# Inverse blocks of the first and last batch turned on VectorE, prologue in another order, joins over four partition groups

## Chip, cores and metric

The kernel runs on one core of a Trainium2 chip. The metric is the device time of one execution in microseconds, taken as the median of several runs. The core has five engines that work from their own queues in order: TensorE (PE, with its weight loads as PEld), VectorE (DVE), ScalarE (ACT), GpSimd (POOL) and SyncE (SP), which here issues all DMAs. They meet only in semaphores.

## What is computed

The input x is 8 batches of 512 tokens with 128 channels in float32. Half a gated feed-forward network (FFN), a gated delta-rule attention block with its own MLP, and half the same FFN again are added to it:

```python
x = x + 0.5 * ffn(layernorm(x))
x = x + attn(layernorm(x))
x = x + 0.5 * ffn(layernorm(x))

# attn: q, k are silu projections of unit length (8 heads of 128), v a silu projection
def step(S, inp):
    q_t, k_t, v_t, a_t, b_t = inp
    kS = jnp.einsum('bhk,bhkv->bhv', k_t, S)
    bk = (b_t[..., None] * k_t)[..., :, None]
    S = a_t[..., None, None] * (S - bk * kS[..., None, :]) + bk * v_t[..., None, :]
    o = jnp.einsum('bhk,bhkv->bhv', q_t, S)
    return (S, o)
```

The FFN is a silu-gated layer from 128 to 512, two gelu layers of 512x512 and one back to 128. All of it stays in float32.

## The kernel before

The recurrence over 512 tokens is cut into NC = 4 chunks of C = 128 tokens. With H = 8 heads that makes U = 32 units per batch, and for each unit a triangular 128x128 system has to be inverted. The inverse ends in R (as left operand of `solve`, line 1537).

**The inverse.** `decayed_k0` and `decayed_k` write the system into R. SyncE's `blocks` sends the four 32x32 diagonal blocks of each unit to `blocks_out`, `blocks_in` brings them back as blkA, now with block and unit (4 x 32) on the 128 partitions. GpSimd's `invert` runs 31 steps of two instructions (lines 580 and 583) on blkT, and then writes the transposed inverse over blkA (line 586). SyncE's `back` sends blkT to t_back and blkA to r_back, waits, and reads them as 32x32 blocks: T into TB by three DMAs, the other into the diagonal of R by four. Four joins on TensorE then build the off-diagonal parts: `join` 0 and 1 work on 32x32 tiles (lines 1873 and 1875), joins 2 and 3 on 64x64 tiles (lines 1881 and 1883). The results of a join lie in banks 6 and 7 (x = 0 and 1, 16 units each), and `joined` on VectorE and ScalarE copies them into TB and R, for the next join and for `solve`. In joins 0 and 1 one bank is filled after the other, and its results alternate between two of the four groups of 32 output partitions.

**The stages.** The order is written out by hand on every engine; nothing is planned by a scheduler. Batch 0 has a prologue, `P_alone`, that exists on every engine: it mixes the first FFN of batch 1 (`f1_slots`, 20 slots), the turns of keys (`turn0(1, c)`) and queries (`turn0(0, c)`), the key products `keys_keys0`, the projections `proj0` and the query products `keys_queries0`. Then come the norm of batch 1 (`N_T`, `N_logits`, `N_sums`), ten projections of batch 1 done ahead (AHEAD) and the four `lone_join`, each with one product of one column ahead of it (`hold`, line 1851). The loop over t = 1 to 5 has the recurrence SP of batch t-1 with the projections of batch t, the first FFN of batch t+1 (`F1`) and the second FFN of batch t-1 (`F2`), between whose slots the joins of batch t stand (JOIN_SLOTS). The last batch's inverse runs beside the second FFN of batch 6, with its joins at LATE_SLOTS 11, 13, 16 and 18, and `SP_tail` follows.

**What waits for what.** In the prologue the first join waits for the three TB DMAs (b_TB), join 1 for the four R DMAs (b_Rin). `SP_first`, the first `solve`, waits for the copies of join 3. `keys_keys` of batch 1 reads KT, which is made by `squares` (VectorE), a power (GpSimd, line 537), `unit_k` (VectorE, lines 811 and 817) and then a store and a load through k_rows. `turn0(0, 0)` waits for `unit_q0(0)`, eight scalings on ScalarE (line 1267) after the reciprocal root of `norms0(0)` on VectorE. TB also holds the gated output of batch 1's first FFN until slot 7 has read it, so VectorE clears a part of it only then (line 898).

## Time and profile before

| | us |
|---|---|
| median of 3 runs (1413.53 to 1416.9) | 1413.98 |
| profiled execution, whole | 1415.69 |
| profiled execution, span | 1414.0 |
| TensorE busy | 1381.2 |
| VectorE busy | 836.1 |
| ScalarE busy | 665.3 |
| GpSimd busy | 570.0 |

The span is the profile's time from the first to the last instruction. A busy time over several stages says little about a single wait: the view of the waits names who ended an idle stretch, the chain shows the steps one after the other, the timeline gives start and length of groups of instructions with the idle time ahead of them, and the view by stretches has the granted clock of TensorE as a share of 2.4 GHz. A float32 matmul appears as two records, so `x128` at line 1873 are 64 matmuls. In the timeline a group's time reaches to the modelled end of its last matmul and overlaps the next group a little; the chain's pieces add up.

### The profile page before, as it was taken

To read this page: it belongs to the slowest core of one execution; us is meant where nothing else is said; L and a number is where in the kernel's file an instruction comes from. 1 tells how busy PE (TensorE), PEld (TensorE's weight loads), DVE (VectorE), ACT (ScalarE), POOL (GpSimd) and SP (SyncE) were. 2 spreads that over 40 slices of the span, in tenths; PEclk is the share of its full clock that TensorE was granted. 3 is DMA by queue.
4 is the path that set the end of the run, shared out by engine and by line. 5 is a ranking of instruction groups with operands and counts; after the bars stand their busy time and mean duration, and the time that the engine had idled before them with its cause. 6 is when DMAs were issued, how large, how long until landed. Compare 5 with 4: busy or idle time off the path is not lost.

```text
span 1414.0 us, 25147 instructions
## 1 busy us (share of the span) xinstructions
PE 1381.2 (98%) x9760; PEld 957.4 (68%) x9760; DVE 836.1 (59%) x2480; ACT 665.3 (47%) x1138; POOL 570.0 (40%) x646
## 2 busy tenths in 40 slices
PE   9999999999999999999999999999999999999998
PEld 5456676657866588566875668656786657864987
DVE  3566677455864566743776548756486445771452
ACT  2567556226652366424573256622566236642233
POOL 0028252831448134561346504284143822566100
PEclk9999999999999999999999999999999999999999
DMA  5120355532554235640447304473155332643000
GB/s 183 55 66 16 89 127 121 95 87 64 133 104 104 52 84 128 119 108 17 119 110 138 86 24 109 103 133 87 41 127 117 79 84 68 146 110 78 17 1 8
DMA packets 359607, 125.00 MB, mean 88 GB/s; under 512 B 325312, under 2 KB 340416, under 8 KB 359488
## 3 DMA queue, kind: packets, MB, share of 16 engines
q1 hardware_dynamic: 359488, 123.40, 37.9%
q8 instruction: 77, 1.26, 0.4%
q14 instruction: 42, 0.34, 0.1%
HBM read 79.58 MB, written 43.78 MB: 87 GB/s over the span
## 4 chain that ended last, share of the span: by engine, by line
PE 77%; POOL 9%; issue 6%; DVE 4%; DMA 2%; ACT 1%; SPq 1%; POOLq 0%; DVEq 0%; ACTq 0%
PE bank L1367 25%; PE bank L1478 9%; PE bank L1396 4%; PE bank L1564 4%; PE bank L1573 4%; PE bank L1537 4%; POOL blkT L583 4%; POOL blkP L580 3%; PE bank L1503 3%; PE bank L1375 3%; PE bank L1554 3%; PE bank L1545 3%; PE bank L1528 3%; PE bank L1520 3%; PE bank L1777 1%
## 5 line engine op out<-in xcount | busy, mean ns | idle before, releaser
L1367 PE MATMUL bank<-big,h 128*128 128x512 f32 (+1 forms) x1056 | 445.9, 571 | 2.3 <-DMA TB<-t_back 2.3
L1367 PEld LDWEIGHTS bank<-big,h 128*128 128x128 f32 x1056 | 195.2, 191 | 194.9 <-issue 186.1
L537 POOL TENSOR_TENSOR rnorm<-ssq,mhalf 128x16 f32<-128x16 f32 (+1 forms) x35 | 84.1, 2403 | 454.4 <-DVE ssq L806 454.4
L1478 PE MATMUL bank<-wqkv,nT 128*128 128x512 f32 x336 | 162.4, 604 | 1.1 <-ACT V L1193 1.1
L583 POOL TENSOR_TENSOR blkT<-blkT,blkP 128x31 f32<-128x31 f32 (+15 forms) x248 | 134.4, 542 | 19.4
L580 POOL TENSOR_TENSOR blkP<-blkA,blkT 128x31 f32<-128x31 f32 (+15 forms) x248 | 129.2, 521 | 32.0 <-DMA blkA<-blocks_out 13.2
L1396 PE MATMUL bank<-xT,w 128*128 128x512 f32 (+1 forms) x272 | 117.2, 573 | 9.2 <-DVE big L707 6.3
L1106 ACT ACTIVATE big<-bank,cols 128x512 f32<-128x512 f32 (+1 forms) x68 | 43.9, 662 | 136.1 <-PE bank L1367 98.2
L1114 ACT ACTIVATE big<-bank,cols 128x512 f32<-128x512 f32 (+1 forms) x68 | 44.0, 661 | 130.0 <-PE bank L1367 130.0
L913 DVE TENSOR_TENSOR MT<-bank,MT 128x512 f32<-128x512 f32 x56 | 38.5, 691 | 100.4 <-PE bank L1520 100.4
L564 POOL TENSOR_TENSOR QET<-QET,sgf 128x1024 f32<-128x1024 f32 x24 | 56.5, 2352 | 102.4 <-DMA sgf<-e_rows 102.4
L1396 PEld LDWEIGHTS bank<-xT,w 128*128 128x128 f32 x272 | 48.7, 190 | 61.1 <-issue 41.5
L1478 PEld LDWEIGHTS bank<-wqkv,nT 128*128 128x128 f32 x336 | 57.8, 194 | 42.6 <-issue 37.6
L546 POOL TENSOR_TENSOR MT<-rows_or_g,maskf 128x1024 f32<-128x1024 f32 x28 | 77.2, 2755 | 13.7 <-PE bank L1564 13.4
L1183 ACT ACTIVATE MT<-MT,biasj 128x128 f32<-128x128 f32 x256 | 78.2, 389 | 0.5 <-POOL MT L546 0.2
L1537 PEld LDWEIGHTS bank<-V,R 128*128 128x128 f32 x512 | 61.5, 192 | 11.7 <-issue 9.8
L1193 ACT ACTIVATE big<-bank 128x512 f32<-128x512 f32 x56 | 32.5, 597 | 77.2 <-PE bank L1478 77.1
L1375 PEld LDWEIGHTS bank<-w,big 128*128 128x128 f32 x512 | 62.5, 192 | 8.6 <-issue 7.9
L1564 PEld LDWEIGHTS bank<-MT,V 128*128 128x128 f32 x512 | 61.3, 192 | 9.6 <-issue 9.6
L1573 PEld LDWEIGHTS bank<-wo,blkA 128*128 128x128 f32 x512 | 61.2, 192 | 8.7 <-issue 8.6
L1375 PE MATMUL bank<-w,big 128*128 128x128 f32 x512 | 66.9, 278 | 0.0
L1520 PEld LDWEIGHTS bank<-QET,KT 128*128 128x128 f32 x448 | 56.4, 192 | 13.4 <-issue 13.4
(221 smaller groups left out, 2458.5 us busy)
## 6 DMA issues: line engine op xcount, KB each, us to landing
rows_or_g<-g_rows SPq DMA_DIRECT2D x28, 512.0 KB, 5.0
q_rows<-mid SPq DMA_DIRECT2D x28, 512.0 KB, 4.9
QET<-q_rows SPq DMA_DIRECT2D x112, 128.0 KB, 4.3
k_rows<-R SPq DMA_DIRECT2D x27, 512.0 KB, 2.8
KT<-k_rows SPq DMA_DIRECT2D x108, 128.0 KB, 3.7
sgf<-e_rows SPq DMA_DIRECT2D x24, 512.0 KB, 4.8
blocks_out<-R SPq DMA_DIRECT2D x128, 32.0 KB, 1.7
blkA<-blocks_out SPq DMA_DIRECT2D x8, 512.0 KB, 3.8
```

The costliest lines, as they stand in the source:

```text
L537: pool.tensor_tensor(rnorm[:, heads_of], ssq[:, heads_of], mhalf[:, :].to_broadcast([128, heads_of.stop - heads_of.start]), ALU.pow).then_ ...
L580: pool.tensor_tensor(prod, A3[:, j, j + 1:].unsqueeze(2).to_broadcast([128, n, m]), T3[:, j:j + 1, 0:m].to_broadcast([128, n, m]), ALU.mul ...
L583: pool.tensor_tensor(T3[:, j + 1:, 0:m], T3[:, j + 1:, 0:m], prod, ALU.subtract).then_inc(b_prod, 1)
L1183: last = act.activation(MT[:, u, :], MT[:, u, :], ACT.Exp, bias=biasj[:, u:u + 1])
L1367: last = pe.matmul(bank[bk + i][:, t], w[:, k, 128 * o:128 * o + 128], src[:, k, t], start=(k == 0), stop=(k == KB - 1))
L1375: last = pe.matmul(bank[4][:, 128 * c:128 * c + 128], src[:, k, 128 * c:128 * c + 128], w[:, k, :], start=(k == 0 and c == chunks[0]), sto ...
L1396: pe.matmul(bank[bk][:, t], w[:, 128 * o:128 * o + 128], xT[:, t], start=True, stop=True).then_inc(f["gate"], 1)
L1478: pe.matmul(bank[proj_bank(b, n)][:, :], nT[:, 128 * c:128 * c + 128], wqkv[:, i // 2, 512 * (i % 2):512 * (i % 2) + 512], start=True, sto ...
L1520: last = pe.matmul(heads(bank[query_bank(b, c, g)])[:, h, :], KT[:, u, :], QET[:, u, :], start=True, stop=True)
L1537: last = pe.matmul(heads(bank[g])[:, h, :], R[:, u, :], V[:, u, :], start=True, stop=True)
L1564: last = pe.matmul(heads(bank[2 + g])[:, h, :], V[:, u, :], MT[:, u, :], start=(c == 0 and h == 0), stop=True, skip_group_check=True)
L1573: last = pe.matmul(bank[2][:, 0:D], oT[:, hh, :], wo[:, hh, :], start=(hh == 0), stop=(hh == H - 1))
```

## The change

Batches 0 and 7 (`turned(b)`) no longer go through t_back and r_back. GpSimd's `invert` ends without the transposed copy, `back` is not called for them on SyncE, and VectorE reads blkT itself by 32x32 block transposes: `turn_T` (one instruction of 128x1024 for the left half of TB), `turn_T1` (32x1024) and four `turn_R` (32x1024 each, one for each diagonal block of R). The joins of these batches wait for b_turn. Joins 0 and 1 of all batches (`join_quarters`) now alternate between banks 6 and 7, and the output groups go round all four: the two banks use different halves. Both banks of such a join are complete at its end only, so `joined` waits for both at k < 2, and reads the group that `at` names. `unit_q0(0)` becomes one VectorE instruction. The rest is order: the third and fourth key turn and the last key products of the prologue come before slots 6 and 7, the first query turn comes after the last slot; join 0 stands before the ahead projections; the norm of xin for batch 2 goes from the joins to the stretch of `decayed_k0`; the squares of batch 1 go before the last copies.

```diff
+def turned(b):
+    return b in (0, B - 1)
...
                 sp.wait_ge(b_prod, b * 2 * (BS - 1) + 2 * (BS - 1))
                 sp.dma_start(t_back.rearrange("p u i c -> (p u) (i c)"), blkT[:, :]).then_inc(b_Tout, 16)
-                sp.wait_ge(b_R, b + 1)
+                sp.wait_ge(b_R, b)
...
-            e_store(0), load_xin(2), load_x1(1), P_alone(), e_load(0, 1), back(0), scaled_rows(0), rows(1), grow_in(1, 0)
+            e_store(0), load_xin(2), load_x1(1), P_alone(), e_load(0, 1), scaled_rows(0), rows(1), grow_in(1, 0)
...
-            P(B - 1), back(B - 1), scaled_rows(B - 1), store(B - 2)
+            P(B - 1), scaled_rows(B - 1), store(B - 2)
...
+                if turned(b):
+                    return
                 pool.wait_ge(b_prod, b * steps + steps)
...
+            def turn_T(b):
+                dve.wait_ge(b_prod, (b + 1) * 2 * (BS - 1))
+                dve.transpose(TB[:, :, 0:BS].rearrange("i u c -> i c u"), T_ci).then_inc(b_turn, 1)
+
+            def turn_T1(b):
+                r = slice(BS, 2 * BS)
+                dve.transpose(TB[r, :, r].rearrange("i u c -> i c u"), T_ci[r]).then_inc(b_turn, 1)
+
+            def turn_R(b, p):
+                r = slice(BS * p, BS * p + BS)
+                dve.transpose(R[r, :, r].rearrange("c u i -> c i u"), T_ic[r]).then_inc(b_turn, 1)
...
+            def joins_alone():
+                turn_T(0), turn_R(0, 1), gates_abs(1), turn_R(0, 3), joined(0, 0)
+                turn_T1(0), joined(0, 1), gates_log(1)
+                turn_R(0, 2), joined(0, 2), turn_R(0, 0), cumulated(1), squares(1, 0), joined(0, 3)
+                N_rows(1, n0, 0, n_n0)
...
-            for k in range(JOINS):
-                joined(B - 1, k)
+            turn_T(B - 1), turn_R(B - 1, 1), turn_R(B - 1, 3), joined(B - 1, 0), turn_T1(B - 1), joined(B - 1, 1)
+            turn_R(B - 1, 2), joined(B - 1, 2), turn_R(B - 1, 0), joined(B - 1, 3)
...
-                turn0(1, 1), keys_keys0(0)
+                turn0(1, 1), keys_keys0(0), turn0(1, 2)
                 f1_slots(5)
-                turn0(1, 2), keys_keys0(1)
-                f1_slots(6)
-                turn0(1, 3), keys_keys0(2)
-                f1_slots(7)
-                keys_keys0(3), proj0(0, 0)
+                keys_keys0(1), turn0(1, 3), keys_keys0(2), keys_keys0(3)
+                f1_slots(6, 7)
+                proj0(0, 0)
...
+            def join_quarters(k):
+                for i in range(16):
+                    col = slice(32 * i, 32 * i + 32)
+                    for x in range(2):
+                        u = 16 * x + i
+                        for e in (0, 64):
+                            e, o = slice(e, e + 32), slice(e + 32, e + 64)
+                            at = (e, o)[(x + k + 1) % 2]
+                            if k == 0:
+                                last = pe.matmul(bank[6 + x][at, col], R[e, u, o], TB[e, u, 0:32], start=True, stop=True)
+                            else:
+                                last = pe.matmul(bank[6 + x][at, col], TB[o, u, 0:32], R[o, u, o], start=True, stop=True)
+                        if i == 15:
+                            last.then_inc(j_full, 1)
```

TensorE's queue in the prologue, from the fourth slot pair on. Lines 1367 and 1414 are slots, 1692 and 1746 turns, 1705 and 1759 the key products, 1676 and 1725 projections. Before:

```order
L1367 MATMUL bank<-TB,h 128x512 x2
L1692 MATMUL bank<-ident,big 128x128 x8
L1705 MATMUL bank<-KT 128x128 x8
L1367 MATMUL bank<-TB,h 128x512 x2
L1692 MATMUL bank<-ident,big 128x128 x8
L1705 MATMUL bank<-KT 128x128 x8
L1367 MATMUL bank<-TB,h 128x512 x2
L1705 MATMUL bank<-KT 128x128 x8
L1676 MATMUL bank<-wqkv,nT 128x512 x2
L1367 MATMUL bank<-big,h 128x512 x2
L1676 MATMUL bank<-wqkv,nT 128x512 x2
```

After:

```order
L1759 MATMUL bank<-KT 128x128 x8
L1746 MATMUL bank<-ident,big 128x128 x8
L1414 MATMUL bank<-TB,h 128x512 x2
L1759 MATMUL bank<-KT 128x128 x8
L1746 MATMUL bank<-ident,big 128x128 x8
L1759 MATMUL bank<-KT 128x128 x16
L1414 MATMUL bank<-TB,h 128x512 x4
L1725 MATMUL bank<-wqkv,nT 128x512 x2
L1414 MATMUL bank<-big,h 128x512 x2
L1725 MATMUL bank<-wqkv,nT 128x512 x2
L1414 MATMUL bank<-big,h 128x512 x2
```

The last key products (with the ones before them a row of 16) now stand ahead of the last two slots that read TB, and the value projections come behind.

VectorE's queue around the first join. Lines 882 and 915 are the query products, 752/754 and 758/760 the gate values, 938 and 982 the copies of join 0; 806 is turn_T, 816 turn_R, 811 turn_T1. Before:

```order
L882 TENSOR_TENSOR MT<-bank,MT 128x512 x2
L730 TENSOR_SCALAR n<-x,lnn_mean,lnn_rs 128x128 x4
L752 TENSOR_SCALAR lz<-bank 128x64
L754 TENSOR_TENSOR absz<-bank,lz 128x64
L762 SCALAR_TENSOR_TENSOR lgb<-bank,lz 128x32
L762 SCALAR_TENSOR_TENSOR lga<-bank,lz 128x32
L771 COPY gT<-bank 32x128
L772 COPY gn<-bank 128x64
L774 TENSOR_TENSOR biasj<-lgb,bank 128x32
L776 TENSOR_TENSOR kdl<-biasj,gn 128x32
L652 BN_STATS lnf_st<-xin 128x6 x4
```

After:

```order
L915 TENSOR_TENSOR MT<-bank,MT 128x512 x2
L806 STREAM_TRANSPOSE TB<-blkT 128x32x32
L816 STREAM_TRANSPOSE R<-blkT 32x32x32
L758 TENSOR_SCALAR lz<-bank 128x64
L760 TENSOR_TENSOR absz<-bank,lz 128x64
L816 STREAM_TRANSPOSE R<-blkT 32x32x32
L982 TENSOR_SCALAR TB<-bank 32x16x32 x2
L811 STREAM_TRANSPOSE TB<-blkT 32x32x32
L984 COPY R<-bank 32x16x32
L985 STREAM_TRANSPOSE TB<-bank 32x16x32
L984 COPY R<-bank 32x16x32
```

The moments and the second row norm went elsewhere; three turns stand around the gate values and the copies of join 0.

TensorE's queue at the joins of the prologue. Lines 1873 and 1932 are join 0, 1875 and 1934 join 1, 1478 and 1525 the ahead projections, 1467 and 1514 the sums of the gates. Before:

```order
L1460 MATMUL bank<-wba,nT 128x16 x4
L1478 MATMUL bank<-wqkv,nT 128x512 x4
L1467 MATMUL bank<-lga,triu 128x32
L1468 MATMUL bank<-lga,ones 128x32
L1469 MATMUL bank<-triu,lga 32x128
L1851 MATMUL bank<-ident 128x1
L1873 MATMUL bank<-TB,R 32x32 x64
L1478 MATMUL bank<-wqkv,nT 128x512 x2
L1851 MATMUL bank<-ident 128x1
L1875 MATMUL bank<-R,TB 32x32 x64
```

After:

```order
L1507 MATMUL bank<-wba,nT 128x16 x4
L1905 MATMUL bank<-ident 128x1
L1932 MATMUL bank<-TB,R 32x32 x64
L1525 MATMUL bank<-wqkv,nT 128x512 x4
L1905 MATMUL bank<-ident 128x1
L1934 MATMUL bank<-R,TB 32x32 x64
L1525 MATMUL bank<-wqkv,nT 128x512 x4
L1905 MATMUL bank<-ident 128x1
L1946 MATMUL bank<-TB,R 64x64 x32
L1514 MATMUL bank<-lga,triu 128x32
```

Join 0 moved ahead of the first four projections, joins 0, 1 and 2 now have four projections between them, and the sums moved behind join 2, with the last two projections ahead of join 3.

## Rows read from the trace of the kernel before

**Rows 1.** Page, busy us with share of the span and number of instructions.
```profile
PE 1381.2 (98%) x9760; PEld 957.4 (68%) x9760; DVE 836.1 (59%) x2480; ACT 665.3 (47%) x1138; POOL 570.0 (40%) x646
```

**Rows 2.** Stretches: length, busy us of five engines, TensorE clock, DMA share, GB/s.
```profile
237.00:400.00 163.00, 163.00 (x1168) 111.44 (x1166) 101.01 (x290) 74.88 (x124) 73.88 (x80) 1.00 0.42 97
147.00:150.00 3.00, 2.94 (x112) 2.92 (x114) 0.68 (x1) 0.59 (x1) 0.00 (x0) 0.64 1.37 164
186.00:189.00 3.00, 3.00 (x11) 2.34 (x11) 2.68 (x3) 0.00 (x0) 0.81 (x1) 0.53 0.03 8
1298.40:1302.00 3.60, 3.60 (x13) 1.31 (x15) 0.00 (x0) 0.73 (x2) 0.00 (x0) 0.56 1.19 198
```

**Rows 3.** TensorE's waits: us in total, times, longest us.
```profile
PE bank L1851 <- DMA TB<-t_back: 2.9, 1, 2.9
PE bank L1503 <- DMA KT<-k_rows: 2.7, 2, 1.8
PE bank L1367 <- DMA TB<-t_back: 2.3, 1, 2.3
PE bank L1692 <- ACT V L1267: 1.9, 1, 1.9
...
PE bank L1460 <- ACT nT L1133: 1.9, 2, 1.0
```

**Rows 4.** Chain in the prologue: start us, us, what.
```profile
93.36 0.70 DVE R L875
...
101.21 0.25 POOL blkP L580
...
138.49 0.25 POOL blkT L583
...
143.24 3.78 DMA TB<-t_back
```

**Rows 5.** Timeline of TensorE, prologue: start us, us, engine, line, operation, idle before.
```profile
139.74 3.68 PE L1478 MATMUL bank<-wqkv,nT 128*128 128x512 f32 x8
...
147.37 3.33 PE L1873 MATMUL bank<-TB,R 32*32 32x32 f32 x128
150.63 3.78 PE L1478 MATMUL bank<-wqkv,nT 128*128 128x512 f32 x4
...
165.66 2.05 PE L1537 MATMUL bank<-V,R 128*128 128x128 f32 x16
```

**Rows 6.** Groups by shape, VectorE and GpSimd: busy us, mean ns, idle before.
```profile
L941 DVE STREAM_TRANSPOSE TB<-bank 32x512 f32<-32x512 f32 x2 | 1.4, 706 | 0.1
...
L817 DVE STREAM_TRANSPOSE R<-big 128x1024 f32<-128x1024 f32 x1 | 1.2, 1245 | 0.0
...
L522 POOL TENSOR_TENSOR KD<-big,kds 128x1024 f32<-128x1024 f32 x3 | 5.6, 1898 | 11.9 <-DVE big L858 11.9
L586 POOL TENSOR_TENSOR blkA<-blkT,ones 128x1024 f32<-128x1024 f32 x1 | 2.5, 2472 | 0.1
```

**Rows 7.** Timelines of VectorE and TensorE around the first KT load.
```profile
173.34 1.22 DVE L811 TENSOR_TENSOR big<-big,rnorm 128x1024 f32<-128x1024 f32 x1 [1.16 <-POOL rnorm L537]
...
184.70 3.18 PE L1503 MATMUL bank<-KT 128*128 128x128 f32 x16 [1.84 <-DMA KT<-k_rows]
187.68 2.44 PE L1478 MATMUL bank<-wqkv,nT 128*128 128x512 f32 x4
```

**Rows 8.** Chain on GpSimd and timeline of TensorE, last batch.
```profile
1289.72 0.25 POOL blkT L583
...
1283.86 12.18 PE L1367 MATMUL bank<-big,h 128*128 128x512 f32 x28
1298.38 3.54 PE L1367 MATMUL bank<-big,h 128*128 128x512 f32 x4 [2.34 <-DMA TB<-t_back]
```

**Rows 9.** Chain, two joins of an inner batch: start us, us, records.
```profile
301.97 2.14 PE bank L1873 x128
...
317.39 2.01 PE bank L1881 x64
```

More of the change, by code:

```diff
@@ L979, in SP_first @@
                 new_state(s, 0, 0)
-                if p is not None:
+                if p is not None and p > 1:
                     squares(p, 0)
@@ L1579, in SP_first @@
                 pe.wait_ge(j_act, s * NA + NA - 1)
+                if turned(s):
+                    pe.wait_ge(b_turn, 12 if s else 6)
                 if p == 1:
@@ L1853, in join_waits @@
             def join_waits(b, k):
+                if turned(b):
+                    pe.wait_ge(b_turn, (6 if b else 0) + (1, 3, 4, 5)[k])
+                if b == 0 and k == 2:
+                    pe.wait_ge(a_TB, 1)
                 if k == 0:
-                    pe.wait_ge(b_TB, b * 3 * 16 + 3 * 16)
+                    if not turned(b):
+                        pe.wait_ge(b_TB, b * 3 * 16)
                     pe.wait_ge(p_dq, b * 2 * NC + 2 * NC)
-                if k == 1:
-                    pe.wait_ge(b_Rin, b * 4 * 16 + 4 * 16)
+                if k == 1 and not turned(b):
+                    pe.wait_ge(b_Rin, b * 4 * 16)
                 if k > 0:
@@ L1884, in join @@
-                    last.then_inc(j_full, 1)
+                        u = 16 * x + i // 2 + 8 * (i % 2)
+                        col = slice(64 * (i // 2), 64 * (i // 2) + 64)
+                        out = (slice(64, 128), slice(0, 64))[(i + k) % 2]
+                        if k == 2:
+                            last = pe.matmul(bank[6 + x][out, col], R[0:64, u, 64:128], TB[0:64, u, :], start=True, stop=True)
+                        else:
+                            last = pe.matmul(bank[6 + x][out, col], TB[64:128, u, :], R[64:128, u, 64:128], start=True, stop=True)
@@ L1886, in lone_join, with join @@
+                    last.then_inc(j_full, 1)
+            def join(k):
+                if k < 2:
+                    join_quarters(k)
+                else:
+                    join_halves(k)
             def lone_join(k):
@@ L1888, in lone_join @@
                 hold(bank[6])
-                join(0, k)
+                join(k)
             pe.wait_ge(c_pool, 1)
```

121 lines of the change are left out of this document (64 added, 57 removed).

## Prediction

> **What bounds the kernel now.** I read the page first. TensorE is busy 98% of the span [rows 1], and in a stretch of two inner batches it is busy 163.00 of 163.00 us at the full clock, 1.00 of 2.4 GHz [rows 2]. So inside the loop only TensorE's own work counts, and what VectorE, ScalarE, GpSimd or a DMA saves is worth nothing there. The second look is at who ends TensorE's waits: a DMA into TB, a DMA into KT, a DMA into TB once more, and ScalarE's scaling of V [rows 3]. The third is the granted clock right behind these waits: 0.64 behind the first, 0.53 behind the second, 0.56 behind the third [rows 2]. 1.2 GHz is the lower level, so work there takes twice as long and each wait is paid about twice. That is the reader's key to this case: three places, each an idle piece plus a slow piece.
>
> All sums are made against the profiled execution, whose span is 1414.0 us. It took 1415.69 in all; the median of the shown runs is 1413.98, so a change of the span is taken off 1414.0.
>
> **Term 1, prologue up to the first solve.** Before, the last update of blkT ends at 138.74; GpSimd turns it for 2.5 us, SyncE then issues, and TB has landed at 147.02 [rows 4]. TensorE ran dry at 144.12, waited 2.9 us, and ran the first join in 3.33 us and the next two projections in 3.78 [rows 3, 5]. Between 139.74 and the first solve at 165.66 lie 25.9 us [rows 5]. The same instructions at the full clock are four projections 3.4, small sums 0.8, four one-column products 0.9, joins 2 x 2.14 + 2 x 2.01, six projections 5.2: 18.6 us. So 7.3 us are lost there, and 1.9 more before the turn of V and 0.9 before the logits (one of the two waits for nT) [rows 3].
>
> Now I lay out the new order with the durations of the trace. TensorE does the last keys-keys block ahead of slots 6 and 7 of the FFN (3.4 us earlier), with one slot and one turn exchanged. VectorE gets 1.7 us of moments in between and still writes the last R at about 91.0 in place of 94.06 [rows 4]. The block DMAs and blkA follow as before (94.06 to 101.1, 7.0 us), the inversion starts near 98.1 and ends at 135.7. The V turn is moved behind the four down slots and scaled on VectorE by about 114.5, three us before it is wanted: the 1.9 us go. I get the logits done at 137.0, with 0.5 us of waiting for the rows of the norm. VectorE comes out of its last query product at 136.8 and turns T until 138.05 (1.25 us for 128x1024, [rows 6]): TensorE waits 1.1 us, too short to fear the clock, since the 1.9 us wait before V was followed by full clock.
>
> Behind it VectorE has R1, the gate values, R3, the copies of join 0, T1, the copies of join 1, and so on. Join 1 needs it at 142.4 and TensorE comes at 143.2 or later: hidden. The last copies stand behind R0, the cumulated gates and the moved squares (2.2 us): TensorE waits about 0.9 us for them. ScalarE's two table changes of the logs now stand between join 0 and join 1, covered by four projections. The sum puts the first solve at 157.6 with joins at today's speed, 8.1 us earlier, and at 156.2, **9.4 us** earlier, with the joins of term 4. SyncE loses the whole back() of this batch; nothing queued there is wanted sooner.
>
> **Term 2, the first KT load.** Before, VectorE made the squares of batch 1 between the two state copies, GpSimd's power followed, and unit_k began at 173.34, 7.7 us after the first solve; KT landed just before 184.70 and TensorE had waited 1.8 us, then ran two groups in 5.3 us where 3.5 is the full-clock time [rows 7]. The squares and the power now lie before the first solve. unit_k follows the state copies at about 4.7 us after the first solve, KT lands at 16.0, and TensorE asks at 17.0. The wait and the slow stretch go: 1.84 + 1.75 = **3.6 us**. Next late is nothing I can see nearer than 1 us.
>
> **Term 3, the last batch.** The last blkT update ends at 1289.97, and TensorE works through its slots until 1296.04 [rows 8]. VectorE has nothing else by then, so T is turned by 1291.3, R1 and R3 by 1293.8, all before TensorE asks. The 2.34 us wait and the slow slot (3.54 us against 1.74, from 14 pairs in 12.18 us) go: **4.1 us**. T1, R2 and R0 lie between joins with two slots (3.5 us) each beside them; the chain of copies ends about 1 us before it is needed.
>
> **Term 4, joins 0 and 1 of batches 1 to 7.** These 14 joins are TensorE's own time. A join of 32x32 tiles takes 2.14 us for 128 records, 16.7 ns each; one of 64x64 takes 2.01 for 64, 31.4 ns each [rows 9]. Both alternate between two output groups. The step of 32 columns costs 14.7 ns, so almost all of the 16.7 grows with the columns that a group must take. The 64x64 form shows that two output groups overlap although they share their rows. With four groups in turn the column part would halve: 2.0 + 7.35 = 9.4 ns, 1.20 us, a saving of 0.94. The other end is nothing, if instructions can't follow faster. Between them stands the slow first join: about 104 of its records ran at the lower level in 2.86 us, 27.5 ns each, which splits 16.7 into 5.9 fixed and 10.8 with the clock; halving the latter gives 11.3 ns, 1.45 us. I take this one, as the nearest row of the same instructions: 14 x 0.69 = **9.7 us**. The copies of the first bank now begin 0.7 us later; three slots of 1.7 us cover that.
> By the Trainium skill, "TensorE: Matmul & The Clock Gate", section on 56 against 53.3 ns, start to start never drops below about 25 ns however small the matmul; by that rule the joins would gain nothing. The trace speaks against it as a bound across tiles, since 16.7 ns is already below. By it the sum would be 1398.2, the first rival.
>
> **Sum:** 9.4 + 3.6 + 4.1 + 9.7 = 26.8; 1414.0 - 26.8 = **1387.2**.
>
> **Rivals.**
> *Joins don't get faster* (the sequencer is the limit at 16.7 ns). For: no row shows four groups, and no record of any kind follows faster. Against: the 14.7 ns that follow the columns. 8.1 + 3.6 + 4.1 = 15.8: 1398.2.
> *The turns are slower.* Their output has a stride of at least 256 bytes, and no VectorE row shows that. For: GpSimd takes 2.47 us for the turned copy and 1.90 for a plain product of that size [rows 6]. Against: the 32x512 turn that writes TB takes 706 ns, about one element a cycle. At 2.4 us each the prologue gets 3.7 us longer, the tail stays covered: 1391.
> "Advanced Engine Details and Errata" of the Trainium skill (SBUF cachelines) says that accesses which all fall into different 16-byte lines pay a penalty; it gives no size. By this rule it would be this case.
> *The inversion does not start earlier,* because keys-keys, copies and VectorE block each other in the new order. T is ready at 140.1, TensorE waits 3.1 us and pays about 2 at the lower clock: 1391.
> *Slower than before: VectorE becomes the bound.* Six turns of t each and 10.0 us of other work stand on it from 136.8 to the first solve, six and 6.2 us in the tail from 1290.0. If they were serial, the first solve falls at 146.8 + 6t and the last at 1296.2 + 6t, where before has 165.7 and 1321.5. With terms 2 and 4 kept, this is break-even at t = 4.8 us, almost four times the row; at 5.6 us it is 1424.
>
> **How the numbers follow.** Forecast 0.48, joins as before 0.27, slower turns 0.12, late inversion 0.08, VectorE as bound 0.05. The range goes from the linear price of the joins (14 x 0.25 and 0.4 less: 1383) to the first rival with 2 us for its turns: 1400. That leaves out the last case, half of the second with the third, and a better prologue. A measurement of this kernel tells about 0.3%, 4.2 us: faster 0.95, same 0.02, slower 0.03.
>
> **What would show it.** The first solve near 156, the TB and KT waits gone from TensorE's list, no stretch under clock 1.0 behind 140 us; the turns at 1.25 us; a join of 32x32 tiles at 1.2 to 1.6 us in the inner batches, 2.14 if the first rival holds. Wrong it would be if TensorE waits over 2 us at join 0, or if a new wait for VectorE appears before joins 1 to 3.

## The result, and the profile after

The changed kernel takes 1397.35 us (median of 4 runs, 1395.63 to 1398.59), the kernel before 1415.02 beside it: a ratio of 0.987, 95% interval 0.986 to 0.989. Its profiled execution spans 1396.0 us, 18.0 less than before's 1414.0. The prediction said 1387.2, range 1383 to 1400: the range held, the point was 8.8 us too low by the spans (10.2 by the medians), and nearly all of that is one term. Of TensorE's waits in the changed kernel (us in total, times, longest) these bear on it:

```profile
PE bank L1759 <- DVE R L908: 3.0, 1, 3.0
...
PE bank L1905 <- DVE TB L806: 2.3, 1, 2.3
PE bank L1584 <- DVE V L996: 1.8, 5, 0.4
PE bank L1550 <- DMA KT<-k_rows: 1.5, 2, 1.0
PE bank L1584 <- DVE R L989: 1.4, 1, 1.4
```

Against [rows 3] both DMA waits for TB are gone and KT's has fallen from 2.7 to 1.5 us. The wait of 1.9 us for V is gone too, as predicted. Two large waits are new: for VectorE's decayed keys in R (L908) and for its turn of T into TB (L806). The first solve, the anchor of term 1, stands at 164.73 us against 165.66 [rows 5]. These rows of TensorE's timeline (start, us, engine, line, operation, idle before) lead up to it. The two stretches under them give length, TensorE's busy time with its records, the granted clock, DMA share and GB/s:

```profile
139.57 0.96 PE L1507 MATMUL bank<-wba,nT 128*128 128x16 f32 x8
142.82 0.56 PE L1905 MATMUL bank<-ident 128*128 128x1 f32 x2 [2.29 <-DVE TB L806]
143.31 1.93 PE L1932 MATMUL bank<-TB,R 32*32 32x32 f32 x128
145.17 5.77 PE L1525 MATMUL bank<-wqkv,nT 128*128 128x512 f32 x8
...
152.20 3.70 PE L1525 MATMUL bank<-wqkv,nT 128*128 128x512 f32 x8
...
164.73 2.05 PE L1584 MATMUL bank<-V,R 128*128 128x128 f32 x16 [1.36 <-DVE R L989]
```
```profile
143.00:147.00 4.00, 4.00 (x132) 0.50 0.39 135
147.00:151.00 4.00, 4.00 (x12) 0.70 0.34 131
```

The same eight projection records take 5.77 us behind the wait, at the lower of the two levels for part of them (0.50 up to 147 us), and 3.70 later. VectorE in the prologue (same columns):

```profile
84.31 1.84 DVE L662 TENSOR_TENSOR lnf_mean<-lnf_st 128x4 f32<-128x4 f32 x1
...
86.15 1.86 DVE L664 TENSOR_TENSOR lnf_tb<-lnf_st 128x4 f32<-128x4 f32 x1
...
88.47 1.29 DVE L908 TENSOR_TENSOR R<-bank,MT 128x512 f32<-128x512 f32 x2
...
140.38 2.18 DVE L806 STREAM_TRANSPOSE TB<-blkT 128x1024 f32<-128x1024 f32 x1
142.59 1.89 DVE L816 STREAM_TRANSPOSE R<-blkT 32x1024 f32<-32x1024 f32 x1
```

The turns take 2.18 and 1.89 us, not the 1.25 of the contiguous turn in [rows 6]. Two four-element operations take 1.84 and 1.86 us; the one of the same form between them (L663, 86.07 us) takes 0.15. GpSimd runs three plain products back to back from before the first to the end of the second (82.38 to 87.99 us):

```profile
82.38 5.61 POOL L526 TENSOR_TENSOR KD<-big,kds 128x1024 f32<-128x1024 f32 x3 [11.71 <-DVE big L884]
```

One join of each size in batch 5 on the timeline, then the first of the last batch (TensorE's loop runs over t = 1 to 6, so batches 1 to 6 have their joins inside it):

```profile
967.80 1.29 PE L1932 MATMUL bank<-TB,R 32*32 32x32 f32 x128
...
982.12 2.08 PE L1946 MATMUL bank<-TB,R 64*64 64x64 f32 x64
```
```profile
1284.04 1.29 PE L1932 MATMUL bank<-TB,R 32*32 32x32 f32 x128
```

In this view a 32x32 join reads 1.29 us, where before's reads 2.21 (978.55 us, L1873); start to start of the neighbours, as in [rows 9], it is 1.22 against 2.14. These 128 records are 64 products. The 64x64 join is what it was. In the last batch join 0 starts at 1284.04 without a wait; before had 2.34 us there [rows 8]. Laid side by side, the kernel gains 0.9 us up to the first solve, 3.9 from there to join 0 of batch 1, 5.9 from there to join 0 of batch 5, and 8.9 from there to join 2 of the last batch, together 19.7 before rounding; then it gives 1.7 back in a slow stretch at 1350 us.

### The profile page after: what moved, and what is told of

Its sections match the earlier page's. It is cut to its first block, busy times and chain, and to the rows that moved or that the text cites. A ratio compares the mean times of both kernels' runs of the same rounds, so it can differ in the third digit from the quotient of the medians.

```text
span 1396.0 us, 25134 instructions
## 1 busy us (share of the span) xinstructions
PE 1364.2 (98%) x9760; PEld 941.7 (67%) x9760; DVE 861.0 (62%) x2493; ACT 662.5 (47%) x1130; POOL 565.3 (40%) x644
## 4 chain that ended last, share of the span: by engine, by line
PE 72%; issue 10%; DVE 8%; POOL 7%; ACT 2%; DMA 2%; SPq 0%; POOLq 0%; DVEq 0%; ACTq 0%
PE bank L1414 22%; PE bank L1525 9%; PE bank L1443 4%; PE bank L1620 4%; PE bank L1584 4%; PE bank L1611 4%; PE bank L1422 3%; PE bank L1550 3%; PE bank L1601 3%; PE bank L1592 3%; PE bank L1575 3%; POOL blkT L587 2%; POOL blkP L584 2%; PE bank L1567 2%; PE bank L1831 1%
## 5 line engine op out<-in xcount | busy, mean ns | idle before, releaser
L550 POOL TENSOR_TENSOR MT<-rows_or_g,maskf 128x1024 f32<-128x1024 f32 x28 | 77.0, 2751 | 12.9 <-PE bank L1611 12.5
L1584 PE MATMUL bank<-V,R 128*128 128x128 f32 x512 | 63.5, 277 | 3.2 <-DVE V L996 1.8
```

Of the source, the lines that this page charges most:

```text
L550: pool.tensor_tensor(MT[:, u, :], grow, maskf[:, :].unsqueeze(1).to_broadcast([128, H, 128]), ALU.add).then_inc(d_mask, 1)
L1584: last = pe.matmul(heads(bank[g])[:, h, :], R[:, u, :], V[:, u, :], start=True, stop=True)
```

## The experiments

Four questions: what are the joins worth and why; what did the turns bring by themselves; what held the prologue; what holds it next. Where a ratio stands, it is to the kernel before on the same chip.

**The joins alone.** The kernel before with the new join loops and their copies:

```
-            def join(b, k):
+            def join_quarters(k):
+                for i in range(16):
+                    col = slice(32 * i, 32 * i + 32)
+                    for x in range(2):
+                        u = 16 * x + i
+                        for e in (0, 64):
+                            e, o = slice(e, e + 32), slice(e + 32, e + 64)
+                            at = (e, o)[(x + k + 1) % 2]
+                            if k == 0:
+                                last = pe.matmul(bank[6 + x][at, col], R[e, u, o], TB[e, u, 0:32], start=True, stop=True)
...
```

> The kernel before with only the joins changed (joins 0 and 1 of all batches over four output groups and alternating banks, and the copies that wait for both banks). Theory 1 (the joins are TensorE time that is saved one to one, 0.92 us each as in the profile after, less a new wait for VectorE's copies of join 1 of 0.2 to 0.75 us in the inner batches): 14 joins save 12.9, new waits cost 2 to 3, so 10 to 11 us, near 1403.5. Rival (the shorter joins only pay together with the new prologue, since every first solve waits for something else): under 5 us, 1409 or more. The join of 32x32 tiles at 1.22 us in either case.

Measured: 1401.2 us (1399.47 to 1401.77), ratio 0.991 (0.988 to 0.993), span 1399.5: 14.5 us less than before's. The first solve is at 166.10 and all three DMA waits stand as before (TB 2.6, KT 2.3, TB 2.2 us), so this is the joins: 14 x 0.92 = 12.9. The other 1.6 come behind the first solve too, where the slow pieces are shorter (the first keys-keys block reads 2.05 us for 3.18, the slot ahead of the last batch's join 0 2.89 for 3.54); what shortens them is not shown. The 10 to 11 us expected were too few: they took off 2 to 3 us of new waits, and the list has 1.1 and 0.3 us for VectorE's TB. Of the 18 us of the whole change the joins are by far the larger part.

**The turns and the prologue alone**, with the join loops and copies of before put back:

```
...
-                join(k)
+                join(0, k)
```

> The changed kernel with the joins of before (two output groups, one bank after the other). Theory 1 (turns, prologue order and squares bring what the profile after shows at its anchors: 0.9 us up to the first solve, less about 1 us of the shorter joins, 3.9 at the first KT load, 4.1 in the last batch): 8 to 9 us below before, near 1406. Rival (the gain of the whole change is nearly all joins and the prologue is worth nothing or a loss): within 4 us of before, 1410 to 1414. The two together should come to the 17.7 us of the change if they are independent.

Measured: 1411.67 us (nine of the ten executions from 1410.4 to 1416.3; the tenth took 6213.5 us and is not in the ratio), ratio 0.998 (0.997 to 1.000), span 1410.2. The rival was right: three of the four terms, 15.8 us by the prediction with joins as before, bring about 4, and 3.8 with the 14.5 of the joins alone is 18.3 against the 18.0 of the whole change, so the two add up. The two new waits of TensorE are in it at full size, 3.0 us for R and 2.3 for TB, and the first solve is at 166.04, no earlier than before.

**The last batch alone** turned by VectorE, in the kernel before:

```
+def turned(b):
+    return b == B - 1
...
```

> The kernel before, with only the last batch's inverse turned on VectorE. Theory 1 (the wait for TB of 2.3 us goes, and the slow slot behind it, 1.8 us): 4.1 us faster, near 1410, and no stretch of lower clock around the first join of the last batch. Rival (the lower clock or a wait comes back a few us later, as the chain of turns and copies of VectorE with turns of 1.9 to 2.2 us runs into joins 2 and 3): 0 to 2.5 us.

Measured: 1413.65 us, ratio 0.999 (0.998 to 1.001): no difference that can be told. Its trace explains why: the wait at the last batch is gone,

```profile
1299.41 2.21 PE L1904 MATMUL bank<-TB,R 32*32 32x32 f32 x128
```

but this execution has a longer low-clock stretch in the prologue, which the edit does not touch: join 1 there reads 3.62 us, the first solve comes at 169.36. From first solve to the last batch's join 0 it is 1130.05 us against before's 1136.19: 6.1 us less, where term 3 said 4.1. The surplus lies elsewhere: from join 0 of batch 6 (1149.74 here, 1147.65 before) to the last batch's join 0 it is 149.67 against 154.20, 4.5 us less, and 0.4 of that is a shorter KT wait (0.53 for 0.90). So this stretch bears out place and size.

**The number of output groups.** First two groups in place of four, the banks still in turn:

```
-                            at = (e, o)[(x + k + 1) % 2]
+                            at = (o, e)[k]
```

> The changed kernel, with one edit in the two joins of 32x32 blocks: each partition group of the input writes to one group of the output only (block 0 to the second group, block 2 to the first), so that two groups of output partitions are in use instead of four. The two banks still take turns from product to product, and the result is the same. It separates two readings of why these joins fell from 2.14 us (before) to 1.22 us (after) for the same 128 products. Theory A (the number of output groups decides): the joins go back to about 2.1 us, 16.7 ns per product, and the span is some 12 us longer than the changed kernel's 1396. Theory B (the taking turns of the two banks decides): they stay at 1.22 us and the span at 1396.

Then four groups inside one bank, all products of one bank ahead of the other's:

```
-                for i in range(16):
-                    for x in range(2):
+                for x in range(2):
+                    for i in range(16):
-                            at = (e, o)[(x + k + 1) % 2]
+                            at = (e, o)[(i + k + 1) % 2]
```

> The changed kernel, with the order of the 128 products of a 32x32 join turned round: all 64 that go to the one bank, then all 64 that go to the other, with four output groups in use inside each bank. The copies behind the joins still expect the old layout, so the decayed key products of two blocks land in each other's places: the output is not the reference's, the work is the same. Theory A (the number of output groups decides): the join stays at 1.22 us. Theory B (the two banks decide): it rises towards 2.1 us. Because the products of all units of half 0 are no longer done first, the copies of half 0 may wait up to 0.6 us longer; in the batches' middle nobody waits for that.

Measured, one execution each: 1413.28 us and span 1411.6 with two groups, 1398.5 and 1396.8 with one bank. The group of the join in a stretch of batch 1, first with two groups, then in one bank (busy us, mean ns):

```profile
L1932 PE MATMUL bank<-TB,R 32*32 32x32 f32 x128 | 2.2, 191 | 0.0
```
```profile
L1932 PE MATMUL bank<-TB,R 32*32 32x32 f32 x128 | 1.3, 194 | 0.0
```

So the banks fall, and the groups decide: two give 16.7 ns a record, four give 9.5, whatever the banks do. One rival stays untested. With four output groups the products also use four pairs of input and output group, with two only two pairs, and no run has four pairs over two output groups. Undoing this alone costs 15.6 us of span, nearly the whole gain. By the Trainium skill, "TensorE: Matmul & The Clock Gate", section "Wait — 56ns, not 53.3ns?", start to start never drops below about 25 ns. A product here is two records, so it costs 33.4 ns with two groups and 19.1 with four: counted by products only the four-group join is below that figure, and it is enough to show that across tiles the figure is no floor.

**What a turn costs.** Nine VectorE turns behind the last work, differing only in stride:

```
+            probe(flat[:, 0:1024].rearrange("p (i c) -> p i c", i=BS), read)
+            probe(flat[:, 0:2048].rearrange("p (c u s) -> p c u s", c=32, s=2)[:, :, :, 0], read)
+            probe(flat.rearrange("p (c u s) -> p c u s", c=32, s=4)[:, :, :, 0], read)
+            probe(flat[:, 0:1024].rearrange("p (u c) -> p c u", u=32), read)
...
```

> The changed kernel plus nine VectorE transposes of 32x32 blocks (32 partitions x 1024 fp32 elements) behind its last work, alone on the chip; they write over values nobody needs any more. They differ only in the stride between neighbouring elements of what is written or read, in this order: contiguous; written with 8 bytes stride; 16 bytes; 128 bytes; 256 bytes; 512 bytes; read with 128 bytes and written contiguous; read with 128 and written with 256 bytes; contiguous again. In the changed kernel the turns that write contiguous units take about 1.25 us and those that write with a stride 1.9 to 2.2 us. Theory A (the stride of the written elements costs): 1 and 9 take 1.25 us, 4 to 6 take 1.9 us or more, 7 takes 1.25 us. Theory B (the turns of the changed kernel are slow because of what runs beside them, GpSimd's port or the running ones): all nine take 1.25 us. Theory C (the stride of what is read costs): 7 and 8 are slow and 4 to 6 are not.

Measured in one execution, in that order: 1232, 1234, 1966, 1895, 1886, 1891, 1892, 2162, 1233 ns. Five of them (count, ns min/median/max, first and last start): 8 bytes, 16 bytes, 128 bytes written, 128 bytes read, both strided.

```profile
L1127 DVE STREAM_TRANSPOSE V<-blkT x1: 1234/1234/1234, 1397.5 to 1397.5; 32x1024 f32<-32x1024 f32 x1
...
L1127 DVE STREAM_TRANSPOSE V<-blkT x1: 1966/1966/1966, 1398.8 to 1398.8; 32x1024 f32<-32x1024 f32 x1
...
L1127 DVE STREAM_TRANSPOSE V<-blkT x1: 1895/1895/1895, 1400.8 to 1400.8; 32x1024 f32<-32x1024 f32 x1
...
L1127 DVE STREAM_TRANSPOSE V<-blkT x1: 1892/1892/1892, 1406.5 to 1406.5; 32x1024 f32<-32x1024 f32 x1
...
L1127 DVE STREAM_TRANSPOSE V<-blkT x1: 2162/2162/2162, 1408.5 to 1408.5; 32x1024 f32<-32x1024 f32 x1
```

Theories A and C are each half right: a written stride of 16 bytes or more costs 0.65 to 0.73 us, a read stride of 128 bytes (the only one tried) 0.66, both together 0.93, and 8 bytes cost nothing. B falls, since nothing else ran. This fits the changed kernel: its R turns in the prologue are strided on one side (1.89 to 1.93 us), its T turns on both (2.18, 2.20). By the Trainium skill, "Advanced Engine Details and Errata", section SBUF Cachelines, at least two accesses must hit a 16-byte line to hide the memory's latency. The step between 8 and 16 bytes is just that; the size, a factor of 1.53 to 1.75, is what these rows add.

**The moments in the prologue.**

```
-                decayed_k0(0)
+                for c in range(NC):
+                    decayed_k0(c)
                 dve.wait_ge(ld_x, 2 * 16 + 16)
                 moments(ln_f["f1"], 2, xin)
-                for c in range(1, NC):
-                    decayed_k0(c)
```

> The changed kernel with one move: the moments of xin for batch 2 stand behind all four products of decayed_k0 and not behind the first, so they no longer meet GpSimd's three scalings of KD (82.4 to 88.0). Theory 1 (two small VectorE additions of 1.84 and 1.86 us in the profile after waited for GpSimd and held back R, and TensorE waited 3.0 us for it): the two take 0.2 to 0.7 us again, the TensorE wait goes, the inversion starts about 3 us earlier, and the kernel is 3 us faster than after, near 1394.5; the first join still waits over 2 us and pays the lower clock. Rival (TensorE's wait for R is set by VectorE's order, not by GpSimd): the wait stays over 1.5 us and the time within 1 us of after.

Measured: 1393.8 us (1391.11 to 1394.51), ratio 0.985 (0.983 to 0.988), span 1389.4. The wait for R has left the list. The small operation is short (VectorE's timeline, then TensorE's):

```profile
91.76 0.17 DVE L662 TENSOR_TENSOR lnf_mean<-lnf_st 128x4 f32<-128x4 f32 x1
```
```profile
139.86 0.56 PE L1904 MATMUL bank<-ident 128*128 128x1 f32 x2 [2.29 <-DVE TB L806]
...
161.84 2.05 PE L1583 MATMUL bank<-V,R 128*128 128x128 f32 x16
```

First solve 2.9 us earlier, the wait for TB untouched. By the time of whole executions the gain over the changed kernel is not clear: the two intervals overlap. The run moved the whole step, so it shows what the step cost where it stood, not why. That the two long operations waited for GpSimd rests on where they lie: with 5.61 us for three products, the products end at 84.25, 86.12 and 87.99, and L662 and L664 run from one end to the next. By the Trainium skill, "SBUF — State Buffer", section "SBUF: two separate sides", VectorE and GpSimd share a port pair that one instruction holds to its end, where VectorE's has two SBUF inputs and GpSimd's reads SBUF. The trace agrees: L662 and L664 each add two SBUF inputs, and beside an idle GpSimd they take 0.17 and 0.16. The trace of the kernel before had the same thing in batch 5, VectorE first, then GpSimd, with both ending at 984.4 us:

```profile
982.44 1.94 DVE L656 TENSOR_TENSOR lnf_mean<-lnf_st 128x4 f32<-128x4 f32 x1
```
```profile
982.01 2.35 POOL L564 TENSOR_TENSOR QET<-QET,sgf 128x1024 f32<-128x1024 f32 x1 [3.80 <-DMA sgf<-e_rows]
```

**The layer norm of the inner batches.** After the change TensorE comes to join 2 earlier, and VectorE's copies of join 1 stand behind a layer norm. The changed kernel in batch 5, VectorE, then TensorE:

```profile
971.49 1.86 DVE L662 TENSOR_TENSOR lnf_mean<-lnf_st 128x4 f32<-128x4 f32 x1
...
976.25 1.12 DVE L677 TENSOR_SCALAR xin<-xin,lnf_mean,lnf_rs 128x128 f32<-128x128 f32 x4
977.28 0.67 DVE L984 COPY R<-bank 32x512 f32<-32x512 f32 x1
```
```profile
980.20 1.98 PE L1414 MATMUL bank<-big,h 128*128 128x512 f32 x4 [0.48 <-DVE TB L985]
```

Join 1 had ended at 975.65; the copies start at 977.28. The first row is again a small addition beside a GpSimd product (970.98 to 973.33).

```
-                joined(t, 0), LN_F1(t + 2), joined(t, 1), joined(t, 2)
+                joined(t, 0), joined(t, 1), LN_F1(t + 2), joined(t, 2)
```

> The changed kernel, with one edit: in every inner batch VectorE's layer norm of the batch after next, which stood between its copies behind join 0 and those behind join 1, stands behind those of join 1. In the changed kernel's trace join 1 of the last inner batch ends at 975.65 us and the copies behind it start only at 977.28, because the layer norm (970.6 to 977.4 us) is ahead of them, and join 2 waits 0.48 us. Theory (the wait that took the place of part of the joins' gain): both waits of that kind (0.38 us at 476.8 and 0.48 at 980.2) go, time 0.9 to 1.5 us less (ratio of the two kernels about 0.999). Rival: the layer norm is then late for GpSimd and the input of the batch after next, or another releaser ends the same wait; no gain, or up to 1 us lost.

Measured: 1395.84 us (1394.39 to 1400.03), ratio 0.986 (0.983 to 0.988), against 0.987 (0.986 to 0.989) of the changed kernel. The waits of that kind are gone from its list, but its KT wait is 2.4 us in place of 1.5. Inconclusive in time: the gain of about 1 us is less than such runs can tell. Its profiled execution was the slowest of the four.

**Three edits of order together:** the two above, and the copies of join 3 ahead of the squares.

```
-                turn_R(0, 2), joined(0, 2), turn_R(0, 0), cumulated(1), squares(1, 0), joined(0, 3)
+                turn_R(0, 2), joined(0, 2), turn_R(0, 0), cumulated(1), joined(0, 3), squares(1, 0)
```

> The changed kernel with three edits of order on VectorE, none of which takes away work: the moments of the next batch's input behind all four decayed-key steps of the prologue (the edit that alone gave 1393.8 us), the layer norm of the inner batches behind the copies of join 1, and the prologue's last copies of join 3 ahead of the squares of batch 1. Theory (the three waits add up): TensorE's 3.0 us wait for R in the prologue and its two waits of 0.38 and 0.48 us for TB in the inner batches go, the 2.29 us wait ahead of join 0 stays, first solve at 161.5 to 162 us, time 1392 to 1393.5 us. Rival: the inner batches' waits turn up behind another releaser and the time stays at 1393.8 or above.

Measured: 1394.37 us (1392.35 to 1394.47), ratio 0.985 (0.983 to 0.986), span 1390.6, first solve at 160.64. No better than the moments alone: 1.2 us won up to the first solve, and KT's waits are 3.3 us where that kernel had 1.2. The rival holds: the releaser is the DMA of KT now, as it was with the layer norm moved alone. The largest of these waits, 1.69 us, is at the first keys-keys block (179.39 us), where the changed kernel waits for nothing. The copies now stand ahead of the squares, which KT is made from: what the edit wins at the solve, term 2 gives back.

**A cover for the first join.** The three edits of order, and three of the ten projections ahead of join 0. This is TensorE's part of the edit; the order of VectorE and ScalarE follows it:

```
+                for c, i in AHEAD[0:3]:
+                    proj(1, c, i)
                 lone_join(0)
-                for c, i in AHEAD[0:4]:
+                for c, i in AHEAD[3:6]:
                     proj(1, c, i)
                 lone_join(1)
-                for c, i in AHEAD[4:8]:
+                for c, i in AHEAD[6:8]:
```

> The kernel with the three edits of order, plus one more: three of the ten projections that TensorE does between the prologue's four joins stand ahead of join 0, so that TensorE has work while VectorE turns T (2.19 us); ScalarE's and VectorE's order follows (logarithms of the gates first). Theory A (the wait ahead of join 0 and the low clock behind it are one loss): the 2.29 us wait goes, the granted clock behind it stays at 2.4 GHz, join 0 takes 1.22 us instead of 1.93 and the projections behind it 0.46 us each instead of 0.7. VectorE then is what the joins wait for: its turns and copies from 136.9 us on add up to 20.9 us (2.2 and 2.2 for T, 4 x 1.9 for R, 7.0 copies, 1.9 for gates and the rest), so the first solve cannot come before some 158 us. First solve at 158 to 159.5 us instead of 161.8, time 1389.5 to 1391 us. Rival B (VectorE's chain already sets the first solve, whatever TensorE does ahead of join 0): first solve still at 161 to 162 us, no gain, the wait moves to joins 1 to 3.

Measured: 1392.65 us (1389.56 to 1393.6), ratio 0.983 (0.981 to 0.985), span 1390.6. Theory A was right up to join 1 and wrong in the number that counts:

```profile
139.90 0.38 PE L1909 MATMUL bank<-ident 128*128 128x1 f32 x2
140.21 1.29 PE L1936 MATMUL bank<-TB,R 32*32 32x32 f32 x128
...
145.29 0.35 PE L1909 MATMUL bank<-ident 128*128 128x1 f32 x2 [1.03 <-issue]
...
150.65 0.35 PE L1909 MATMUL bank<-ident 128*128 128x1 f32 x2 [1.87 <-DVE TB L984]
...
161.01 2.05 PE L1586 MATMUL bank<-V,R 128*128 128x128 f32 x16
```
```profile
152.00:156.00 4.00, 4.00 (x46) 0.50 0.02 6
```

Join 0 comes without a wait at the full clock. Then TensorE, with work taken from the later gaps, waits 1.0 and 1.9 us ahead of joins 1 and 2; the low clock has moved behind these, and the first solve is at 161.01 against 160.64 without the cover. As rival B said.

**The cover spread** by what VectorE needs: 2, 4, 4 and 0 projections, in place of 3, 3, 2 and 2.

```
+                for c, i in AHEAD[0:2]:
+                    proj(1, c, i)
                 lone_join(0)
-                for c, i in AHEAD[0:4]:
+                for c, i in AHEAD[2:6]:
                     proj(1, c, i)
                 lone_join(1)
-                for c, i in AHEAD[4:8]:
+                for c, i in AHEAD[6:]:
                     proj(1, c, i)
                 lone_join(2), N_sums(1)
-                for c, i in AHEAD[8:]:
-                    proj(1, c, i)
                 lone_join(3)
```

> The last kernel (three edits of order and projections ahead of join 0), with its ten projections spread by what VectorE needs: two ahead of join 0, four between joins 0 and 1, four between joins 1 and 2, none between joins 2 and 3 (there it was 3, 3, 2, 2), and on VectorE the gates' sums ahead of the last turn of R. In that kernel TensorE waited 1.0 us ahead of join 1 and 1.9 us ahead of join 2, the granted clock fell to 0.50 from 152 us on, and the first solve stood at 161.0 us, no earlier than the 160.6 us without the cover. Theory A (it was the waits' place: work before join 2 keeps TensorE busy and the clock up): no wait over 0.9 us ahead of joins 0 to 2, granted clock 1.00 from 144 to 156 us, first solve at 158 to 159 us, time 1.5 to 2.5 us below 1392.7 us. Theory B (VectorE's 20.9 us of turns, copies and gates set the first solve in any order): the waits turn up again ahead of join 3 or the solve, first solve at 160 us or later, no gain.

Measured: 1390.53 us (1389.26 to 1392.23), ratio 0.982 (0.980 to 0.984): the best of the versions that do all the work, its interval clear of the changed kernel's. Waits ahead of the joins are 0.67, 0.19, none and 0.18 us, and from 144 to 156 us the clock is 1.00:

```profile
144.00:156.00 12.00, 11.50 (x224) 1.00 0.15 47
```
```profile
137.66 0.96 PE L1506 MATMUL bank<-wba,nT 128*128 128x16 f32 x8
...
158.68 3.78 PE L1583 MATMUL bank<-V,R 128*128 128x128 f32 x16 [0.24 <-DVE R L988]
```

From the logits (L1506) to the first solve it is 21.0 us, against 24.8 with the first cover and 24.1 with none. Theory A holds in its numbers; what VectorE still sets is in the next run. The solve itself then ran at the lower clock (3.78 us for 2.05), which gives 1.7 back.

**The turns made contiguous**, in that kernel:

```
+                if b == 0:
+                    dve.transpose(blkA[:, :].rearrange("q (i c) -> q i c", i=BS), T_ic).then_inc(b_turn, 1)
+                    return
...
```

> The same kernel as e11_spread, but the six turns of the prologue read and write contiguous rows of a tile that is idle then, in place of the strided places in TB and R: the turned blocks of batch 0 never reach TB and R, so the output is not the reference's; every join, copy and wait stays. It measures what the strides of the turns cost in the prologue. By the turns measured alone (contiguous 1.23 us; 1.89 us with one side strided; 2.16 us with both) six turns take 7.5 us in place of 12.0. Theory B above (VectorE sets the first solve): it comes 3.5 to 4.5 us earlier than in e11_spread, at 154.5 to 156 us, where TensorE's own 17.4 us of joins, projections and sums behind 137.2 us become the bound. Theory A (TensorE's waits and clock set it): first solve less than 2 us earlier than in e11_spread.

Measured: 1387.49 us, span 1385.8, one execution. Its output is not the reference's.

```profile
137.84 0.96 PE L1517 MATMUL bank<-wba,nT 128*128 128x16 f32 x8
...
156.53 2.05 PE L1594 MATMUL bank<-V,R 128*128 128x128 f32 x16 [0.34 <-DVE R L999]
```

Logits to first solve 18.7 us, 2.3 less than with strided turns. VectorE saved 4.7 us in six turns (7.5 for 12.2); only half of it was on the path. It lies between both theories: above A's 2 us, short of B's 3.5. VectorE now waits 1.57 us for join 1 itself, and TensorE's last wait is 0.34 us: TensorE's own work is the bound. Of the 4.7 us between the two spans, 1.7 is the solve, which ran at the full clock here.

## Why the prediction came out as it did

That the time lies in the range is in part luck. It lies near the upper end, which was laid out for joins that get no faster and turns of 2 us. The joins got faster than forecast; what brought the time there is term 1, so the range held for another reason than its own. The prediction named two signs of being wrong. One came: TensorE waited over 2 us at join 0 (2.29). The other, a new wait for VectorE ahead of joins 1 to 3, is absent in the prologue, and inner batches have 0.38 and 0.48 us one slot ahead of join 2. Of the signs of being right, the DMA waits for TB went and the join of 32x32 tiles came within its 1.2 to 1.6 us, but the first solve was not near 156, the clock behind 140 us fell to 0.50, and no turn took 1.25 us.

**Term 1 (predicted 9.4, came to 0.9) failed, in three steps that the runs tell apart.** The prediction had the logits at 137.0 and the first solve 19.2 us behind. The trace has 139.57 and 25.2. With the 1.9 us wait for V gone, the logits still came 0.7 us later than before (138.83).

*"VectorE gets 1.7 us of moments in between and still writes the last R at about 91.0."* The durations were those of places where GpSimd was idle, and the step was moved beside three of its products. Moments took 5.0 us (83.42 to 88.47), the last R was written at 94.1, TensorE waited 3.0, and all behind it came some 3 us later. Moving them behind the products of R, which were then done at 90.95, gave 2.9 at the first solve. The price of the neighbour stood in the trace of before, at 982.44 us.

*"Turns T until 138.05 (1.25 us for 128x1024)."* The turn is strided on both sides, 2.18 us; with the R turns the strides are 2.3 us on the path (contiguous turns, above). The prediction had this as a rival, priced it at 2.4 us each and 3.7 in all, and gave it 0.12. It should have been the forecast: every turn added was strided, and the row taken for its price was not.

*"TensorE waits 1.1 us, too short to fear the clock."* It waited 2.29, and the clock fell to 0.50: join 0 took 1.93 us in place of 1.29, the projections behind it 5.77 in place of 3.70. In the version with spread projections, where wait, low clock and the late last copies are gone, 21.0 of the 25.2 us remain, and 18.7 without strides: about the 19.2 of the prediction. So its account of TensorE's work fits, as far as versions with another order can tell, and its account of VectorE's was not right.

The third rival, "the inversion does not start earlier", named the symptom but not the whole cause: VectorE was held by its own moments, stretched by GpSimd, more than by keys-keys and copies. The wait behind the squares was seen, 0.9 predicted and 1.36 measured. The last rival had the right engine, at a size that did not make the kernel slower: its formula for a serial VectorE, 146.8 + 6t, gives 159.0 with the six turns' mean of 2.03 us, and the version with spread projections comes to 158.7. With contiguous turns (1.24) it gives 154.2 where 156.5 was measured, so it holds only as long as VectorE is the bound. In the first cover's run it was VectorE that kept the first solve at 161.

**Term 2 (3.6) was right:** 3.9 us from the first solve to join 0 of batch 1. TensorE comes to the first keys-keys block and does not wait:

```profile
181.64 1.95 PE L1550 MATMUL bank<-KT 128*128 128x128 f32 x16
```

"Next late is nothing I can see nearer than 1 us" was not right: the kernel before already waits 0.90 us for KT in a late batch (1198.72 us), and the changed one 0.51 and 0.96.

**Term 3 (4.1) was right.** Join 0 starts without a wait, and the copy chain keeps ahead. Its size was right too. Join 0 of batch 6 and of the last batch, before and then after:

```profile
1147.65 2.21 PE L1873 MATMUL bank<-TB,R 32*32 32x32 f32 x128
...
1301.85 2.21 PE L1873 MATMUL bank<-TB,R 32*32 32x32 f32 x128
```
```profile
1135.79 1.29 PE L1932 MATMUL bank<-TB,R 32*32 32x32 f32 x128
...
1284.04 1.29 PE L1932 MATMUL bank<-TB,R 32*32 32x32 f32 x128
```

That is 154.20 against 148.25 us, 5.95 less; the two joins in between are 1.84 of it, and 4.1 are left.

**Term 4 (9.7) was too small:** 14 x 0.92 = 12.9. The prediction had 1.20 us at its linear end and took 1.45 by a split of the slow first join into a fixed and a clocked part; 1.22 was measured. The runs let the split be made again, since a whole first join ran at a granted clock of 0.50 with four groups (143.31 to 145.17 us in the changed kernel, 1.86 us) and with two, in the run of the turns alone, 3.56 us:

```profile
143.32 3.62 PE L1930 MATMUL bank<-TB,R 32*32 32x32 f32 x128
146.88 4.85 PE L1523 MATMUL bank<-wqkv,nT 128*128 128x512 f32 x8
```
```profile
143.30:147.00 3.70, 3.70 (x130) 3.62 (x130) 3.58 (x4) 0.60 (x2) 1.14 (x1) 0.50 0.41 138
```

A record of two groups takes 27.8 ns there and 16.7 at the full clock, one of four groups 14.5 and 9.5. As an estimate from these four, two groups have 5.6 ns fixed and 11.1 with the clock, four groups 4.5 and 5.0. So the split was right (5.9 and 10.8), and so was halving its second part; wrong was that the fixed part would stay, as it fell as well. The first rival, joins no faster, falls. The prediction set 16.7 ns against the 25 ns of the Trainium skill. That argument was weaker than it read: 16.7 ns is a record, and a product of two records took 33.4 before.

Four batches brought 5.9 in place of 7.4. The changed kernel has new waits in them, 0.38 us for VectorE's copies and 0.51 for KT, and 0.48 more in batch 5. These do not simply belong to shorter joins: with the joins alone the same four batches brought 7.7.

**Summed by the spans:** term 1 8.5 short, term 2 0.3 over, terms 3 and 4 together 1.1 over, 1.7 lost late: 8.8 short, which is the miss.

## What to carry to other kernels

Small TensorE products are worth spreading over all four output groups before anything is moved off a DMA; here that alone was 13 to 15 of 18 us. When a DMA's work is given to an engine, price it with a row of the same strides on both sides. When a step is moved beside another engine's work, take its price from a row with the same neighbour. Work to cover a wait is taken from somewhere: count what each gap needs first, since a cover in the wrong gap only moved the wait and the low clock.

## Of the hardware, not expected

- A 32x32 float32 product costs 19.1 ns start to start (two records of 9.5) over four output groups and 33.4 (two of 16.7) over two. With four groups it makes no difference whether the banks take turns or all products of one bank go first.
- A VectorE turn of 32-bit elements costs 1.23 us per 1024 elements with a written stride of up to 8 bytes, 1.89 to 1.97 with 16 bytes or more written or 128 read, 2.16 with both. Turning 128 partitions takes as long as 32 (2.18 against 2.20).
- In the late tail the same instructions behind the same waits (0.47, 0.39, 1.32 us) ran at a granted clock of 0.89 over 15 us in some profiled executions and at 1.00 in others, which is the 1.7 us given back late. The place in the span does not decide it: with the third wait ending at 1352.71 us, the probe's run had 0.89 and the one-bank run 1.00. What does stays open. The solve at 158.68 us, behind waits of 0.2 us, ran at the lower clock too.
